# Cross attention and ternary feed-forward on one core: four blocks with barriers against one block whose stages follow each other

## What is computed

```
q = (layernorm(x) @ Wq);  k, v = split(ctx @ Wkv)          # 32 heads of 16
q, k = axial_rope(q, pos), axial_rope(k, pos)
w = softmax(q k^T / 4);  attn = w v
x = x + attn @ Wout + bout
# bitlinear(a, w): a = layer_norm(a), absmax-quantised to +-128 per row,
#                  w = sign(round(w / mean|w|)) * mean|w|
h = gelu(bitlinear(layernorm(x), w_fc))                     # 512 -> 2048
x = x + bitlinear(h, w_proj)                                # 2048 -> 512
```

## Time and profile before

| | |
|---|---|
| time, median of 3 runs | 890.2 us (888.17 to 891.32) |
| profiled execution | 892.17 us, its span 890.4 us |
| mean granted TensorE clock | 0.967 |
| busy share of PE, DVE, ACT, POOL | 93%, 80%, 52%, 41% |
| busy share of PE's weight loads | 41% |
| DMA, bytes moved | 94.36 MB, 106 GB/s mean |
| project, about | 0 to 148 us |
| attend, about | 148 to 549 us |
| mix, about | 549 to 656 us |
| ffn, about | 656 to 890 us |

### The profile page before, as it was taken

How to read it: one execution, slowest core, us unless ns; L and a number is a source line. 1 busy time by engine, 2 the same in 40 slices (tenths; PEclk the granted TensorE clock), 3 DMA queues, 4 the chain that set the end, 5 groups by cost and what they waited for, 6 DMA issues and landing times. The chain is left out here.

```text
span 890.4 us, 15912 instructions
## 1 busy us (share of the span) xinstructions
PE 825.2 (93%) x4290; PEld 367.5 (41%) x4290; DVE 711.7 (80%) x970; ACT 460.8 (52%) x873; POOL 362.1 (41%) x512
## 2 busy tenths in 40 slices
PE   1899995999999999999999997999669999999996
PEld 0788882232333333333333322565324444444442
DVE  4888875888888888888888852799949999998892
ACT  3576662377777777777777775233333112122110
POOL 2488876544444444444444420677711111011010
PEclk9999996599999999999999999999969999999998
DMA  7378886333332333343223202343004365454363
GB/s 250 99 207 246 238 228 152 95 96 97 86 85 79 95 95 84 95 95 93 81 78 93 83 1 76 113 142 94 13 1 73 81 119 107 83 106 100 76 119 83
DMA packets 136134, 94.36 MB, mean 106 GB/s; under 512 B 77088, under 2 KB 116000, under 8 KB 136096
## 3 DMA queue, kind: packets, MB, share of 16 engines
q1 hardware_dynamic: 136096, 93.90, 42.2%
HBM read 55.85 MB, written 16.78 MB: 82 GB/s over the span
## 5 line engine op out<-in xcount | busy, mean ns | idle before, releaser
L771 DVE TENSOR_REDUCE attend_maxima<-attend_banks 128x2 f32<-128x1024 f32 x256 | 301.7, 1220 | 64.9 <-PE attend_banks L696 64.7
L794 ACT ACTIVATE attend_probs<-attend_banks 128x512 f32<-128x512 f32 x512 | 271.9, 596 | 84.7 <-PE attend_banks L728 84.7
L728 PE MATMUL attend_banks<-stacks_q_stack,stacks_k_stack 98*128 98x512 bf16 x512 | 175.6, 386 | 2.0 <-ACT attend_probs L794 1.8
L696 PE MATMUL attend_banks<-stacks_k_stack,stacks_q_stack 96*128 96x512 bf16 x512 | 161.1, 398 | 6.8 <-PEq L151 4.5
L738 PE MATMUL attend_banks<-attend_probs,attend_v_ones 128*32 128x512 f32 x1024 | 137.3, 608 | 1.5 <-ACT attend_probs L794 1.0
L1252 ACT ACTIVATE kept_o_all<-ffn_banks,kept_row_scale 128x512 f32<-128x512 f32 x64 | 44.0, 687 | 147.6 <-PE ffn_banks L1217 139.4
L1230 PE MATMUL ffn_banks<-kept_wT,kept_o_all 128*128 128x512 f16 x512 | 115.3, 385 | 4.8 <-DMA kept_o_all<-kept_o_all 4.8
L1217 PE MATMUL ffn_banks<-kept_wT,kept_uT 128*128 128x512 f16 x512 | 114.8, 384 | 1.4 <-PEq L870 1.4
L728 PEld LDWEIGHTS attend_banks<-stacks_q_stack,stacks_k_stack 98*128 98x128 bf16 x512 | 39.5, 97 | 140.5 <-ACT attend_probs L794 85.5
L1331 POOL TENSOR_SCALAR ffn_powers<-ffn_moments 128x1 f32<-128x1 f32 x16 | 17.5, 1091 | 180.4 <-DVE ffn_moments L1269 180.4
L829 POOL TENSOR_SCALAR attend_neg_max<-attend_maxima 128x16 f32<-128x16 f32 x32 | 8.3, 259 | 188.5 <-DVE attend_maxima L771 188.5
(11 more groups left out here) (147 smaller groups left out, 1091.9 us busy)
## 6 DMA issues: line engine op xcount, KB each, us to landing
k_parts<-kept_wT SPq DMA_DIRECT2D x48, 128.0 KB, 3.0
q_parts<-kept_wT SPq DMA_DIRECT2D x48, 128.0 KB, 2.4
stacks_q_stack<-q_parts SPq DMA_DIRECT2D x32, 192.0 KB, 3.0
stacks_k_stack<-k_parts SPq DMA_DIRECT2D x96, 64.0 KB, 2.6
stacks_k_stack<-k_parts SPq DMA_DIRECT2D x32, 192.0 KB, 2.7
kept_o_all<-in_x_dram SPq DMA_DIRECT2D x16, 256.0 KB, 3.4
kept_o_all<-in_L_ffn_w_fc_dram SPq DMA_DIRECT2D x16, 256.0 KB, 3.2
kept_o_all<-in_L_ffn_w_proj_dram SPq DMA_DIRECT2D x16, 256.0 KB, 5.1
```

Of the source, the lines that this page charges most:

```text
L696: mm = nc.tensor.matmul(score_slot[j % 2][:, i], q_stack[0:STACK, slot, head, c * P:(c + 1) * P], k_stack[0:STACK, slot, head, :], start=T ...
L728: nc.tensor.matmul(banks[:, ST_BANK[k]], k_stack[0:STACK + 2, slot, head, c * P:(c + 1) * P], q_stack[0:STACK + 2, slot, head, :], start=T ...
L771: dve.tensor_reduce(maxima[:, at.slot(2), 2 * j:2 * j + 2], score_slot[j % 2], AX.X, ALU.max).then_inc(scores_read, 1)
L794: nc.scalar.activation(probs[:, c, head, :], banks[:, ST_BANK[k]], ACT.Exp, scale=1 / math.sqrt(HEAD)).then_inc(exp_done, 1)
```

## The change

All four stages stand in one block, written out without hardware loops, and every engine goes from one stage to the next by semaphores alone. The attention part keeps its groups and its order on PE. What is different beside that:

- **v through DRAM.** ACT writes v of a tile into a padded tile between ones (`save_v`), SP stores it (`store_v`, 512 KB in pieces of 512 B) and loads it per group (`load_v`). Three groups' parts and v are loaded, and a fourth group's parts, inside the last steps of project. POOL's copy of v goes.
- **Sums through DRAM.** ACT, not DVE, copies the bank of sums after the fifth exponential of a step; SP stores it and loads two groups at once so that the weighted sums fill one 128x512 tile and the sums of weights, each repeated 16 times, another. DVE inverts the second tile, POOL multiplies. The transposes of mix go.
- **Ternary weights** are turned by a DMA each (`turn_weight`), not by PE and ACT; so are the rows u (`turn_u`).
- **One loop for rows.** Output projection, quantisation of u, feed-forward and finish of different tiles share a step. ACT, not DVE, subtracts the mean of h, in one instruction of 2048 columns.

The diff, cut to its core (new code; what it replaces is described above):

```diff
+    def store_v(self, sp, n):
+        sp.wait_ge(self.v_saved, n + 1)
+        sp.dma_start(self.mem.v_padded.rearrange("b g p c e -> b c p g e")[n // CHUNKS, n % CHUNKS],
+                     self.v_pad[:, n % 2].rearrange("p (g e) -> p g e", g=HG)).then_inc(self.v_stored[n % 2], DMA)
...
+    def turn_weight(self, sp, n):
+        sp.wait_ge(self.ternary_ready, n + 1)
+        sp.dma_start_transpose(self.mem.wT[:, n].rearrange("p (k r) -> p k r", k=KX), self.ternary[:, n % 2]
+                               ).then_inc(self.wT_turned[n % 2], DMA)
+    def store_sums(self, sp, g):
+        sp.wait_ge(self.o_saved, g + 1)
+        sp.dma_start(self.mem.o_rows[g], self.o_ring[:, g % O_SLOTS]).then_inc(self.o_stored[g % O_SLOTS], DMA)
+    def load_sums(self, sp, pair):
+        for g in (2 * pair, 2 * pair + 1):
+            sp.wait_ge(self.o_stored[g % O_SLOTS], (g // O_SLOTS + 1) * DMA)
+        need(sp, self.divided, pair - 1)
+        rows = self.mem.o_rows[2 * pair:2 * pair + 2].rearrange("g (j t d) q -> t (g j) d q", t=2, d=HEAD)
+        for to, t in ((self.numer, 0), (self.sums, 1)):
+            sp.dma_start(to[:, pair % 2], rows[t]).then_inc(self.sums_loaded[pair % 2], DMA)
...
+    def weigh_v(self, pe, g, c):
+        pe.wait_ge(self.exp_done, g * 16 + GH * (c + 1))
+        if c == 0:
+            pe.wait_ge(self.v_loaded[g % V_SLOTS], (g // V_SLOTS + 1) * DMA)
...
+            need(pe, self.o_saved, g)
...
+    def invert_sums(self, dve, pair):
+        r = pair % 2
+        dve.wait_ge(self.sums_loaded[r], (pair // 2 + 1) * 2 * DMA)
+        dve.reciprocal(self.sums[:, r], self.sums[:, r]).then_inc(self.inverted, 1)      # 128x512
+    def save_sums(self, act, g):
+        need(act, self.o_stored[g % O_SLOTS], g // O_SLOTS * DMA)
+        act.wait_ge(self.pv_done, (g + 1) * CHUNKS)
+        act.copy(self.o_ring[:, g % O_SLOTS], self.pv_bank).then_inc(self.o_saved, 1)
+    def divide(self, pool, pair):
+        pool.wait_ge(self.inverted, pair + 1)
+        pool.tensor_tensor(self.attnT[:, pair], self.numer[:, pair % 2], self.sums[:, pair % 2], ALU.mult
+                           ).then_inc(self.divided, 1)
...
+    def turn_u(self, sp, n):
+        sp.wait_ge(self.u_ready, n + 1)
+        need(sp, self.fc_ready, (n - U_SLOTS + 1) * QUARTERS)
+        sp.dma_start_transpose(self.uT[:, n % U_SLOTS], self.u_parts[:, n % 2].rearrange("p t c -> p (t c)")
+                               ).then_inc(self.u_turned[n % U_SLOTS], DMA)
...
+    def centre_h(self, act, n):
+        act.wait_ge(self.h_stats_ready, n + 1)
+        now = self.h[:, n % H_SLOTS, :]
+        act.activation(now, now, ACT.Identity, bias=self.h_moments[:, n % 2, 0:1], scale=-1.0
+                       ).then_inc(self.h_centred, 1)
```

The order of each engine's list, from the one block (stages project and rows shortened to what is new in them):

```diff
+        # SP, project, for s in range(TILES + 6): loads of tile s and pieces of s-2 as before, then
+                if within(s - 4, TILES):
+                    prj.store_v(sp, s - 4)
+                if within(s - 5, TILES) and (s - 5) % 2 == 1:
+                    prj.store_parts(sp, s - 5)
+                if 12 <= s < 16:
+                    att.load_stacks(sp, s - 12)
+                if 13 <= s < 16:
+                    att.load_v(sp, s - 13)
+        # SP, attend, for s in range(GROUPS + 5): load_weight(s), load_stacks(s), store_sums(s-4),
+        #   load_sums((s-5)//2) where s-5 is odd, load_max(s-2), load_v(s-1), turn_weight(s-2);
+                if s == GROUPS + 2:
+                    rows.load_x(sp, x, 2)
+                    rows.turn_u(sp, 0)
+        # SP, rows, step s: load_x(s+3), turn_h(s-1, 0), turn_u(s+1), turn_h(s-1, 1), store(s-3)
...
+        # PE, between the stages
+            att.scores(pe, 0, 0)
+            prj.turn_rotated(pe, TILES - 1, 0)
+            att.scores(pe, 0, 1)
+            prj.turn_rotated(pe, TILES - 1, 1)
+            att.scores(pe, 0, 2)
+            prj.add_totals(pe)
+            for j in range(3, 2 * GH):
+                att.scores(pe, 0, j)
+            for s in range(1, GROUPS + 3):
+                att.tensor_step(pe, s)
+                if s in (GROUPS, GROUPS + 1):
+                    rows.mix(pe, s - GROUPS)
+        # PE, rows, step s: expand(s, 0..3), mix(s+2), contract(s-2)
...
+        # DVE, attend and the passage to rows
+            for s in range(1, GROUPS):
+                for j in range(2 * GH):
+                    if j == 4 and s >= 6 and s % 2 == 0:
+                        att.invert_sums(dve, (s - 6) // 2)
+                    att.row_maxima(dve, s, j)
+            att.invert_sums(dve, PAIRS - 3)
+            rows.add_residual(dve, 0)
+            att.invert_sums(dve, PAIRS - 2)
+            rows.quantise_u(dve, 0)
+            rows.add_residual(dve, 1)
+            att.invert_sums(dve, PAIRS - 1)
+        # DVE, rows, step s: finish(s-3), add_residual(s+1), clip_h(s-1), quantise_u(s+1),
+        #   second_h(s-1), statistics(s)
...
+        # ACT, attend
+                for k in range(16):
+                    if within(s - 2, GROUPS):
+                        att.exponentials(act, s - 2, k)
+                    if k == 4 and within(s - 3, GROUPS):
+                        att.save_sums(act, s - 3)
+                    if k == att.HALFWAY - 1 and within(s - 1, GROUPS):
+                        att.save_max(act, s - 1)
+                if s == GROUPS + 1:
+                    rows.centre_u(act, 0)
+        # ACT, rows, step s: centre_h(s-1), activate(s, 0), centre_u(s+1), activate(s, 1..3)
...
+        # POOL, attend, step s: divide((s-7)//2) where s is odd, ternarise(s), split_maxima(s)
```

More of the change, by code:

```diff
@@ L47 @@
 GROUPS = BATCH * HG
+PAIRS = GROUPS // 2
 GW = GH * HEAD
@@ L58 @@
 PI_BELOW = 3.1415925
[L59 to L88, removed]
@@ L91, in run_steps @@
[L91 to L101, removed]
+DMA = 16
+PAIR_STORES = DMA * 2 * 2 * PARTS
+STACK_SLOTS = 4
+STACK_LOADS = DMA * 7
+INPUT_SLOTS = 4
+QUARTERS = FFN // DIM
+V_SLOTS, O_SLOTS = 3, 3
+X1_SLOTS, H_SLOTS, U_SLOTS = 6, 4, 3
@@ L104, in need @@
 def need(eng, semaphore, value):
-    if not isinstance(value, int) or value > 0:
+    if value > 0:
         eng.wait_ge(semaphore, value)
[L110 to L129, removed]
@@ L132, in load_stacks @@
[L132 to L144, removed]
@@ L223, in project, with xattn_ffn, sem @@
+def xattn_ffn(nc, x, ctx, pos, wq, wkv, wout, bout, w_fc, w_proj, out):
+    with ExitStack() as stack:
+        def sem(name):
+            return stack.enter_context(nc.semaphore(name))
+        mem = Memory(nc, stack)
+        prj = Project(nc, mem, sem)
+        att = Attend(nc, mem, prj, sem)
+        rows = Rows(nc, mem, att, sem)
+        filled, pads_set = sem("filled"), sem("pads_set")
+        within = lambda n, count: 0 <= n < count
         block = stack.enter_context(nc.Block())
@@ new lines, in _ @@
+            for s in range(TILES + 3):
+                if 3 <= s + 3 < TILES:
+                    rows.load_x(sp, x, s + 3)
+                if within(s - 1, TILES):
+                    rows.turn_h(sp, s - 1, 0)
+                if s + 1 < TILES:
+                    rows.turn_u(sp, s + 1)
+                if within(s - 1, TILES):
+                    rows.turn_h(sp, s - 1, 1)
+                if within(s - 3, TILES):
+                    rows.store(sp, out, s - 3)
+            for i in range(2):
+                sp.wait_ge(rows.out_stored[i], TILES // 2 * DMA)
@@ new lines, in _ @@
+            att.scores(pe, 0, 0)
[10 more added lines that the diff above has]
+                    rows.mix(pe, s - GROUPS)
+            for s in range(TILES + 2):
+                if s < TILES:
+                    for o in range(QUARTERS):
+                        rows.expand(pe, s, o)
+                if s + 2 < TILES:
+                    rows.mix(pe, s + 2)
+                if within(s - 2, TILES):
+                    rows.contract(pe, s - 2)
```

1974 lines of the change are left out of this document (948 added, 1026 removed).

## The result

| | before | after |
|---|---|---|
| time, median | 889.7 us (888.17 to 891.32, 4 runs) | 921.1 us (918.55 to 923.46, 4 runs) |
| ratio to before, 95% interval | | 1.0352 (1.0319 to 1.0386) |
| profiled execution's span | 890.4 us | 919.2 us |
| mean granted TensorE clock | 0.967 | 0.963 |
| DMA, bytes moved | 94.36 MB | 132.40 MB |

What follows compares the result with a forecast made beforehand. The prediction took PE to bound project, attention and feed-forward, and DVE to bound mix. Its terms -2.5 + 13 - 3.4 + 54 - 45 = +16 on the median of 890.2 gave 906 us, range 872 to 927.

Steps and rivals of the forecast that it cites:

- Start: Kernel start: the first DMA no longer waits behind the first barrier, so it is issued some 2.5 us earlier; -2.5.
- Project: Project stage: SP's fuller issue list delays the last x, +10, and a lower clock adds +3; +13, between 0 and +22.
- Rival (c): Project: the DMA engines are the bound, +17 rather than +10, total 913 us; chance 0.09.
- Into attention: Project to attention: scores start at once, -6.2, but raw weights load late and POOL makes ternary values first, +2.8; -3.4.
- Attention: Attention stage: weights' turning leaves PE, -7.4, waits for the copy, +27, and for reciprocals, +34.5; together +54.
- the copy: Attention: PE waits 0.87 us a group for ACT to copy out the bank of sums, 31 groups; +27.
- the reciprocal: Attention: a 3.3 us reciprocal on DVE every second step makes PE wait 2.65 us, 13 times; +34.5.
- (a): Attention: the reciprocal is cheap or hidden, -34.5 or up to -38, total 872 or 868 us; chance 0.10.
- (b): Attention: the copy of the sums makes nobody wait, 27 us fall away, total 879 us; chance 0.11.
- (d): Attention: a reciprocal takes 4.3 us, PE waits 3.6 rather than 2.65 us, total 921 us; chance 0.08.
- Rows: Output projection and feed-forward in one loop: PE's step 17.3 us, 298.4 us against 343.3 from the last exponential; -45.
- (e): Rows loop: DVE, not PE, sets the step; at 18.3 us a step the total is 919 us; chance 0.08.

Runs made afterwards that it cites:

- p5: Changed kernel with the two stores of each part of q and k made one issue of 128 partitions, into a new DRAM layout; 1024.7 us.
- p3: Changed kernel with four loads of stacks and three of v moved behind the last load of x in SyncE's list; 921.4 us.
- p1: Changed kernel with the sixteen stores of v issued by ScalarE instead of SyncE; 915.7 us.
- p4: Changed kernel with the two feed-forward weight pieces loaded per tile in project half as wide, in as many issues; 920.3 us.
- r1: Changed kernel with the thirteen reciprocals inside attention's steps inverting one column of 512; 885.1 us.
- x1: Changed kernel with both edits: thirteen reciprocals of one column, and VectorE copying the bank of sums between maxima 0 and 1; 860.8 us.
- c1: Changed kernel with VectorE, not ScalarE, copying the bank of sums between maxima 0 and 1, for groups 0 to 28; 916.7 us.
- c3: c1 with each of the thirteen reciprocals split into two of 256 columns, one in each of two steps; 885.3 us.

## Why the prediction was right in sign and short in size

- **Start**, -2.5. Right: ACT's first copy starts at 7.15, 3 us earlier than before.
- **Project**, +13, the step that failed. PE's last projection ends at 160.0, not 138.1: +22, or +25 beside the start's gain, which is beyond the term's own bound of 22. The mechanism was the one named, SyncE's list: p5 shows it as long as no stack is loaded, p3 shows the stacks' share (7 us on the last x), and p1 gives back 5.4 for 16 issues. Mis-sized was the price of the issues. For two tiles the prediction reckoned 8.4 us for twelve stores of parts (0.7 each), 4.4 for eight loads and 1.5 for two stores of v, 14.3 in all, from a trace whose SyncE had gaps. Measured before the stacks came, the stores took 9.9 and 9.5 (the first four 3.94 and 4.15 rather than 2.99, the others 0.64 to 0.66 each but for one pair), the loads 5.2 and 6.2, and v's stores only 1.0: 16.1 and 16.8. With two stacks and a v it was 22.7, where 14.3 and 6.8 were reckoned. What lengthens some issues of the same DMA and not others is open. Rival (c), the DMA engines, would have been nearer in size (+17 for +10), but falls as the bound: half the weights' bytes bought 0.8 us (p4), and the engines carried 312 GB/s when asked (p5). Whether full engines stretch single issues no run decides.
- **Into attention**, -3.4. Nearly right: 184.1 - 160.0 = 24.1 us to the first transposed scores, 29.0 before, -4.9. The source of its +2.8, the raw weights at the end of SyncE's list, is what ties attention's start to that list. The first transposed scores of the kernel before, in order of time, and of the changed one:

```profile
167.07 0.63 PE L728 MATMUL attend_banks<-stacks_q_stack,stacks_k_stack 98*128 98x512 bf16 x1
```

```profile
184.12 0.63 PE L610 MATMUL banks<-stack_words 98*128 98x512 bf16 x1
```

- **Attention**, +54. Right: from the first transposed scores to the last exponential's end 435.4 us (184.12 to 619.5) against 380.0, +55. By part: turning -0.23 a step, as said (23.67 to 23.22 in two); the copy 0.79 a step, not 0.87 (24.79 - 23.22, halved); the reciprocal 2.5, not 2.65. Together -7 + 24 + 33 = +50. (The prediction's own lengths, 312.0 - 309.66 + 0.25, give 2.59 for the reciprocal's wait, not the 2.65 that it summed.) Of the other 5, the half clock behind the first reciprocal is 4.5, which no term had; 3.4 is an output projection that now lies in this stretch, at 604.00, and that the prediction counted with the rows; and against them the first steps run at half clock for 3 us instead of 8 (184 to 187; before 167 to 175.5), -3 by that estimate. Rivals (a) and (b) fall with r1 and x1. The reciprocal took 3.34 us, not the 4.3 that were estimated from the Trainium skill's repeat count ("VectorE: DVE Perf Modes", § Walkthrough: the 8-slice pipeline in each mode), so (d) falls: 3344 ns for 512 columns and 1743 for 256 are 6.25 ns a column. That (d)'s time, 921, is the one measured is chance.
- **Rows**, -45. Nearly right: from the last exponential's end to the end 299.7 us, where 295 was forecast (298.4 less the 3.4 that lie ahead of it). PE's step is 17.3 us (659.79 to 677.05, two starts of `expand`) without idle, so (e) didn't come. The passage is 5 us longer: the second `expand` waits 7.0 us rather than 3, both first ones run at a lower clock.

By these terms the two profiled spans differ by 28.8 us (919.2 - 890.4) where the sum had 16: project is 12 of the 13 that are missing, the passage 5, and the start, the way into attention and attention are together 4 better than reckoned. The medians differ by 31.4.

What the prediction had no term for, beside that, is an interaction. It summed copy and reciprocal as two delays; taken away one at a time they are worth 4.5 and 36.0, together 60.4.

## What to carry to other kernels

A queue's issues can cost more in a fuller list than in the trace they are priced by (12.8 us reckoned, 15.1 to 15.8 measured for the same twenty): add up the whole list per tile, leave room, and look at what stands last in it. A stall that is longer than its engine's slack is cheaper in two pieces than in one. When a repair removes a wait and the time stays, look at the granted clock of the stretch behind the neighbouring wait before giving the repair up.

## What the runs showed of the hardware

- The same 2.34 us wait of PE was followed by 3.4 us at 1.2 GHz in c1, each time in steady attention, and in the changed kernel by 10 us at 1.2 GHz the first time and by none the other twelve times. In c1 PE had a 0.72 us wait less in each step ahead of it; but the changed kernel's first wait has the 0.72 us waits ahead of it too, so this is not the whole difference. Why the clock falls behind one such wait and not behind another is open; none of c3's waits of 0.74 us was followed by a lower clock (1.00 from 190 to 560 us).
- The first four `k_parts` stores of two tiles took SyncE 2.99 and 3.07 us in the kernel before (at 99.53 and 112.28), which has gaps in its queue, and 3.65 to 4.15 from 60 to 100 us in the changed kernel, which has none; most later ones took 0.64 to 0.66 each in both. Six stores of 512 pieces each (p5, from 59.6 us) took SyncE 5.6 us, where twelve of 256 pieces had taken 9.7 (from 60.2 us).
- In p5 three loads of `q_parts`, two of them from sources of several runs with gaps between, held SyncE for 1.8 to 8.4 us, where the same bytes from one run took 1.3 to 3.0; the 8 KB of `max_rows` behind such loads are what PE waits for in attention. Which part of the path is slow is open.
